# Two graph layers on one core: 128-column mask products in two of five row groups, and the kept sums reloaded in seven pieces

## What is computed

```python
h = relu(layernorm(x))
scores = (h @ W @ a1)[:, None] + (V @ W @ a2)[None, :]
e = where(adj > 0, leaky_relu(scores, 0.2), -9e15)
x = x + elu(softmax(e, axis=1) @ V + h)
h = relu(layernorm(x))
x = x + relu((adj.T @ h) @ U.T / adj.sum(axis=0)[:, None])
```

## Time and profile before

| | us |
|---|---|
| median of 3 runs | 379.76 |
| lowest, highest | 377.72, 380.29 |
| the profiled execution | 379.21 |
| its span, first to last instruction | 377.4 |
| mean granted TensorE clock, as a share | 0.959 |

### The profile page before, as it was taken

The page is one execution under the profiler, slowest core; times in us unless marked ns, Lnnn a source line. Parts: engine busy times, 40 slices in busy tenths (PEclk is TensorE's granted clock), DMA queues, the critical chain, the costliest instruction groups (busy, mean ns, idle before and its releaser), DMA issues.

```text
span 377.4 us, 16296 instructions
## 1 busy us (share of the span) xinstructions
PE 304.1 (81%) x7582; PEld 280.0 (74%) x7582; DVE 302.5 (80%) x410; ACT 257.4 (68%) x323; POOL 117.6 (31%) x120
## 2 busy tenths in 40 slices
PE   1927766657778777777888999999979999999995
PEld 0812655556667766677788999888969999999995
DVE  7899999797999558888997879999969876402965
ACT  2222799779999789698999899997767787101000
POOL 8866387388140382030106103003101110401000
PEclk9977699889999899899999999999999999999999
DMA  9999999999999999997101002000321000510211
GB/s 164 137 111 106 110 107 111 137 107 109 109 110 139 104 109 105 103 102 82 58 3 34 24 24 80 24 24 25 129 59 30 5 3 3 112 31 2 55 33 30
DMA packets 27961, 27.88 MB, mean 74 GB/s; under 512 B 22169, under 2 KB 23129, under 8 KB 27766
## 3 DMA queue, kind: packets, MB, share of 16 engines
q0 software_dynamic: 4752, 16.90, 43.1%
q1 hardware_dynamic: 20982, 9.39, 10.0%
q10 hardware_dynamic: 2160, 0.56, 0.8%
HBM read 74.08 MB, written 3.43 MB: 205 GB/s over the span
## 4 chain that ended last, share of the span: by engine, by line
PE 38%; DVE 25%; ACT 22%; issue 9%; DMA 4%; POOL 1%; SPq 1%; DVEq 0%; POOLq 0%
DVE scratch L895 15%; PE w L1248 12%; ACT q L745 10%; PE q L1335 9%; ACT arena L727 9%; PE q L1221 8%; DVE arena L947 5%; PE w L1335 4%; DMA bi<-rows_sb 3%; ACT arena L731 3%; PE w L1120 1%; DMA buf_a<-in_L_gnn_a_dram 1%; PE w L1294 1%; POOL buf_a L517 1%; SPq L420 1%
## 5 line engine op out<-in xcount | busy, mean ns | idle before, releaser
L1248 PE MATMUL w<-v_sb,arena 128*61 128x65 f32 (+1 forms) x4224 | 158.7, 225 | 7.9 <-issue 6.5
L895 DVE CUSTOM_DVE_ANT_0 scratch<-adj_sb,t_row 125x2048 uint8<-125x2048 uint8 x66 | 152.9, 2317 | 1.5
L1248 PEld LDWEIGHTS w<-v_sb,arena 128*61 128x61 f32 (+1 forms) x4224 | 143.6, 140 | 9.7 <-issue 7.6
L1221 PE MATMUL q<-bi,adj_sb 128*64 128x125 bf16 x2112 | 95.8, 226 | 38.8 <-ACT q L745 27.2
L1221 PEld LDWEIGHTS q<-bi,adj_sb 128*64 128x64 fp8e4 x2112 | 71.4, 113 | 53.6 <-ACT q L745 36.3
L727 ACT ACTIVATE arena<-q,t_col 128x1000 f32<-128x1000 f32 (+2 forms) x102 | 88.4, 870 | 7.5 <-PE q L1221 7.4
L731 ACT ACTIVATE arena<-arena,t 128x1000 f32<-128x1000 f32 (+2 forms) x58 | 63.6, 1096 | 23.2 <-DVE arena L947 22.6
L947 DVE SCALAR_TENSOR_TENSOR arena<-arena,b_col,q 128x1000 f32<-128x1000 f32 (+1 forms) x43 | 52.3, 1224 | 19.4 <-PE q L1221 14.6
L745 ACT ACTIVATE q<-second_row,minus_b 128x750 f32<-128x750 f32 (+1 forms) x49 | 47.9, 977 | 1.1
L745 ACT ACTIVATE q<-arena,minus_b 128x375 f32<-128x375 f32 (+1 forms) x53 | 42.3, 800 | 1.3
L1335 PE MATMUL q<-g_all,adj_sb 124*128 124x129 f16 (+1 forms) x588 | 34.8, 220 | 0.0
(11 more groups left out here) (144 smaller groups left out, 229.6 us busy)
## 6 DMA issues: line engine op xcount, KB each, us to landing
adj_sb<-in_adj_dram POOLq DMA_DIRECT2D x33, 500.0 KB, 39.3
t_row<-saved_dram SPq DMA_DIRECT2D x1, 1290.0 KB, 7.2
saved_dram<-x_sb SPq DMA_DIRECT2D x6, 193.5 KB, 1.9
arena<-s_dram SPq DMA_DIRECT2D x2, 500.0 KB, 7.2
out_dram<-v_sb SPq DMA_DIRECT2D x10, 96.0 KB, 1.8
x_sb<-in_x_dram SPq DMA_DIRECT2D x1, 928.0 KB
v_sb<-x_dram SPq DMA_DIRECT2D x1, 768.0 KB, 5.7
v_sb<-n_L_gnn_entity_embs_dram ACTq DMA_DIRECT2D x2, 256.0 KB, 5.6
```

Of the source, the lines that this page charges most:

```text
L895: nc.vector.tensor_tensor_reduce(out=junk[0:R, :], in0=adj_bytes[0:R, b, half], in1=t_row[0:R, half], scale=1.0 / ONE, scalar=0.0, op0=ALU ...
L1221: last = nc.tensor.matmul(q[n % Q_SLOTS][e:e + width, bank, start:start + R], weights, bi[:, i % BI_SLOTS, k, :], start=not ON_ACT[n] and ...
L1248: last = nc.tensor.matmul(att(i)[e0:e1, bank, place_in, :], e[:, k * R + e0:k * R + e1], v_sb[:, c, :], start=(c == 0 and place_in == 0), ...
```

## The change

The constant `MASK_COLUMNS` becomes 128 for groups 1 and 2, so that a block's mask takes one weight load and one matmul. The reload of the saved sums is cut into seven transfers, the k-th of which waits for the attend of tile 2 + 4k of the last group (`weighed` counts the attends, 128 of them in groups 0 to 3). DVE waits for all seven.

```diff
-    MASK_COLUMNS = (64, 64, 64, 64, 64)
+    MASK_COLUMNS = (64, 128, 128, 64, 64)
...
+    LOAD_TILES = (2, 6, 10, 14, 18, 22, 26)
...
             save(SAVES[0] + SAVES[1], SAVES[2])
             sp.wait_ge(part_saved, 16 * len(AHEAD))
             sp.wait_ge(r1_ready, NI)
-            sp.dma_start(saved, saved_dram).then_inc(part_loaded, 16)
+            for k, o in enumerate(AHEAD):
+                first, size = k * 3 * (2 * D + 1), (OUTS[o][1] - OUTS[o][0]) * (2 * D + 1)
+                sp.wait_ge(weighed, NC * (NI - 1) + LOAD_TILES[k])
+                sp.dma_start(saved[:, first:first + size], saved_dram[:, first:first + size]).then_inc(part_loaded, 16)
...
                     if o == AHEAD[0]:
-                        dve.wait_ge(part_loaded, 16)
+                        dve.wait_ge(part_loaded, 16 * len(AHEAD))
```

## The result

The changed kernel takes 372.62 us (median of 4 runs, 372.29 to 373.14) against 379.25 us for the kernel before, timed beside it (377.72 to 380.29): a ratio of 0.984, with a 95% interval of 0.981 to 0.987. The span of the profiled execution went from 377.4 to 370.5 us.

A forecast was written before the change was run, and what follows sets the result against it. PE was taken to be short of instructions, whose packets queue behind adjacency data, not of array time. Terms: -5.6 (holes) + 0.9 (width changes) - 2.0 (reload) = -6.7 us, forecast 372.7 us, range 369.2 to 376.8.

The forecast's parts named there:

- the forecast's own case: Whole kernel: the summed gain arrives, 372.7 us, within its own range of 370.0 to 374.8; chance 0.60.
- the first masks of groups 2 and 3: Signs in PE's trace: group 2's first mask at 133.9 us instead of 135.2, group 3's near 197.
- End of group 1: A 1.66 us hole delays a DVE tile and idles ACT 1.28; removing it gains 1.3 us.
- Group 2: Without PE's holes, DVE's mask waits shrink: 3.7 us gained up to tile 12, 1.0 at tile 18.
- a remaining hole: Group 2, tiles 7 to 11: tiles would outrun instruction feeding at 1.91 us each, leaving a 0.4 us hole.
- three changes of width: PE switching between mask and attend widths costs about 0.25 us a tile where nothing covers it.
- Group 4: Last group: cutting the reload removes the 2.02 us hole at 274.70; gain 2.0, bounds 2.0 and -3.6.
- a seventh hides, seven times, gain 2.0: Reload in group 4: each piece's 0.6 us delay fits within PE's instruction slack, so the whole 2.0 us is gained.
- The size of a piece: Reload: each 193.5 KB piece needs about 0.6 us for its data, likened to a save landing in 1.9 us.
- feeding would still bind in group 2: Rival: instruction supply still limits group 2, half of its 4.7 us stay, 375.1 us; chance 0.17.
- another engine would catch the gain: Rival: DVE, nearly full late in group 2, limits it; 2 to 3 us less gain, 375.5 us; chance 0.07.
- The slower rivals: Width changes dearer than in group 3, up to 385 us, or seven small reload holes, 378.3; chance 0.04 each.

The follow-up runs named there:

- pad: Changed kernel plus idle one-column weight loads behind each wide mask, restoring the instruction count of before; 379.04 us, ratio 0.999.
- nostream_64: Kernel before (64-column masks, one-piece reload) with adjacency blocks 17 to 32 filled with ones by GpSimd, not loaded; 373.17 us, ratio 0.986.
- reload_only: Changed kernel with masks back at 64 columns everywhere, keeping the seven-piece reload; 377.17 us, ratio 0.996.
- mask_only: Kernel before with 128-column masks in groups 1 and 2, keeping the one-piece reload; 371.9 us, ratio 0.982.
- nostream_128: 128-column masks in groups 1 and 2, one-piece reload, adjacency blocks 17 to 32 filled with ones instead of loaded; 372.77 us, ratio 0.985.
- phase_one: Wide masks in groups 1 and 2, one-piece reload, plus 192 idle weight loads in group 0 to move block boundaries; 373.34 us, ratio 0.985.
- burst_64: Kernel before, 64-column masks, with the reload's seven pieces issued one behind the other without waiting for tiles; 376.63 us, ratio 0.994.
- phase_seven: Changed kernel plus 192 idle weight loads in group 0 to move block boundaries; 372.56 us, ratio 0.984.
- wide_both12: Changed kernel with attend also wide (one piece of 125 columns) in groups 1 and 2; executions of 452.71, 497.88, 497.94 and 499.06 us.
- wide_g1: Kernel before with 128-column masks in group 1 alone, one-piece reload; 375.74 us, ratio 0.991.

## Why the prediction was right, and where it was not

**The time.** Predicted 372.7, measured 372.62; the span fell by 6.9 where the sum had 6.7. The chance given to the forecast's own case was 0.60, and it is the case that came. That the sum came so close is luck in part: the term for the start was 0.35 too large, those for groups 2 and 4 were 0.35 and 0.2 too small, and one of them had the wrong cause. Of the signs named, the first masks of groups 2 and 3 came at 134.25 and 197.41 us, against 133.9 and 197, and no hole of PE was left.

**What bounds.** The reading of the holes as PE short of instructions, 256 to a packet, held under both tests: they come back with the number of instructions (pad), and go with the stream (nostream_64). The Trainium skill (Runtime: NRT & Kernel Launch, "Instruction fetch mechanics") has blocks of 256 instructions, which the holes of before, reload_only and pad bear out, 256 apart or nearly. That crossing one is mostly hidden holds in nostream_64 from 100 us to the reload and in group 3 of every kernel, and not beside a full DMA, where holes of up to 2.27 us stood. So what decided the prediction was to ask of ACT's long unbroken chain why it had holes, and not of PE's busy time.

**The terms.**
- End of group 1: predicted 1.3 us, less one change of width, measured 0.7 at group 2's first scores. In `mask_only` it is 1.1. DVE's guard passes set the start of that stretch and ended 0.46 us later in the trace of after (122.65 against 122.19) than before. So the small transfers were issued only 0.90 us earlier (127.83 against 128.73) instead of 1.3. The term was too large by what DVE lets through.
- Group 2: predicted 3.7 + 1.0 - 0.4 for a remaining hole - 0.65 for three changes of width = 3.65; measured 4.0. No hole remained, though it was close. If a block can be run 2.2 to 2.5 us after its packet begins to move, as at the holes before, those of 150.64 and 156.56 us were there just when PE crossed, or up to 0.15 and 0.4 us before it (152.99 and 159.18). This is an estimate from these rows. The price of the widths was near: 0.28 a cycle (1.64 against 1.36) for the 0.25 predicted, and 1.12 for the group (nostream_128 against nostream_64) where the forecast had 0.65.
- Group 4: predicted 2.0, measured 2.2. **Here the cause was wrong.** The sum put this gain to the seven pieces, as a term beside that of the masks. mask_only has the gain without them. The step that failed is "a seventh hides, seven times, gain 2.0": it took it as given that the one piece would cost its hole again in the changed kernel. The two terms weren't independent: fewer instructions also move the block boundary, and a hole of this kind is there or not by less than 0.1 us (0.60 in phase_one, 0.66 in nostream_64). The seven pieces do cure the hole where there is one, as reload_only and burst_64 show (2.2 us); beside the wide masks they had nothing to cure. The trace of before gave a hint: the earlier trace rows has one hole in the last group, in a stretch where a boundary comes every 3.7 us, so that what falls on it was bound to be chance.
- The size of a piece: the estimate of 0.6 us for its data was too low. A piece landed after 2.5 us instead of 1.9, and its data moved from 0.94 to some 2.06 us after its issue, 1.1 us. That was still too little to hold PE.

**The rivals.** That feeding would still bind in group 2 did not come: PE had no hole, and DVE waited 0.34, 0.21 and not at all in the first half. By the estimate above it was a near miss. That another engine would catch the gain did not either: group 3 is 61.52 to 61.54 us in every kernel of the table, so it passes on whatever it gets. The slower rivals are out by PE's cycle of 1.64, and by group 4 in the changed kernel and in phase_seven.

**The small transfers ahead of group 2** took 5.5 to 6.1 us in all these kernels with a stream. What follows them varies more: in phase_one PE had idled 2.11 us for them, and the first mask of group 2 then took 1.02 us, with a granted clock of 0.52 for 2 us; in mask_only it had idled 1.70 and the mask took 0.63. The length of the idle time does not decide it alone, for in phase_seven it was 2.11 us as well and the clock stayed at 1.00. Group 2's first scores vary from 135.99 to 138.01 us among kernels with the same masks in groups 1 and 2. Between mask_only and phase_one this is all of the 2.0 us by which their spans differ.

**What stays open.** Why an instruction packet waits behind data already queued was not looked into; the runs show only that it does, and when. Nor is it known why the granted clock fell behind some idle times of PE and not behind others.

## What to carry to other kernels

An idle time that nothing is shown to end, and that comes back in an engine's timeline at equal counts of its instructions, points at an engine waiting for its own code. Take it from the timeline: the chain's rows called "issue" are not enough, for those of 2.18 us, in both kernels, stand where DVE is busy with a guard pass. Then look at what fills the DMA at that time, and save instructions rather than work. Cut a large transfer that falls into a stretch bound by such an engine; here it helped even without spreading. And when two edits each cure a stall of this kind, do not add them: each moves the places where the other's stall would fall, so run each alone before giving it the credit.

## What the runs showed of the hardware that was not expected

- TensorE's granted clock stood at 0.50 (1.2 GHz) in wide_both12 from 150 to 200 us, while PE was busy 50.00 and its weight loads 49.47 of 50.00 us. All of that stretch lies in group 2, where attend's products were wide. In group 1, with the same wide products, it was still 1.00 from 90 to 100 us. Before it fell, at 137 us, PE had stood idle for 1.15 us at the start of group 2.
- The granted clock also fell right behind some holes: its mean was 0.71 in the block after the hole of 2.27 us in the kernel before, and 0.57 in the 4.0 us after a hole of 1.25 us in burst_64 (at 172.92). In wide_g1 it stayed at 1.00 behind holes of 1.81, 1.80 and 2.05 us.
- A transfer of 1.29 MB holds back an instruction packet until 3.6 to 4.5 us after the boundary if PE crosses it 0.66 to 0.76 us after the transfer's issue, and not at all at 0.60. Seven transfers for the same data, all issued within 4.28 us, let it through 1.2 us after the boundary.
- The holes ended 2.2 to 2.5 us after their instruction packet began to move, those beside the adjacency stream (147.37 to 149.61 before) and those beside the reload (274.54 to 276.72) alike.
- A weight load of one column isn't free: in pad, attend starts 0.69 us after the mask (150.05 to 150.74) with 16 such loads between them, against 0.56 (142.03 to 142.59) without.
